# Second layer's experts on sorted token tiles, and attention's mask added by VectorE

## What is computed

```python
a = a * decay + ekv_t          # scan over t, once forwards, once in reverse
b = b * decay + ek_t
num = nf + nb - ekv + euk * vf
den = df + db - ek + euk
out = sigmoid(r) * (num / maximum(den, 1e-8)) * (0.8 + 0.2 * tf)
```

## Time and profile before

| | |
|---|---|
| Median of 3 runs | 1093.78 us (1093.57 to 1094.86) |
| The profiled execution | 1093.23 us, span 1091.4 us |
| TensorE, weight loads | 867.0 us (79%), 668.0 us (61%) |
| VectorE | 675.6 us (62%) |
| ScalarE | 416.4 us (38%) |
| GpSimd | 312.0 us (29%) |
| DMA | 46.51 MB, mean 43 GB/s |

### The profile page before, as it was taken

How to read it: one execution, slowest core, us unless ns; L and a number is a source line. 1 busy time by engine, 2 the same in 40 slices (tenths; PEclk the granted TensorE clock), 3 DMA queues, 4 the chain that set the end, 5 groups by cost and what they waited for, 6 DMA issues and landing times. The chain is left out here.

```text
span 1091.4 us, 12660 instructions
## 1 busy us (share of the span) xinstructions
PE 867.0 (79%) x4116; PEld 668.0 (61%) x4121; DVE 675.6 (62%) x1194; ACT 416.4 (38%) x869; POOL 312.0 (29%) x244
## 2 busy tenths in 40 slices
PE   0677564777888862545999999999997799999996
PEld 0233353655666542235778878887886778888884
DVE  6887896379999988664456555555555333232324
ACT  3201422322323215765445445445444243433432
POOL 0310001135556533421101101100100145555553
PEclk9888796789999995876899999999999599999999
DMA  3000001111211003003011011000000143233331
GB/s 123 1 1 1 0 1 59 69 49 49 84 61 49 20 0 135 0 1 111 6 39 40 1 40 38 15 23 0 0 0 2 58 119 89 57 97 78 82 69 39
DMA packets 31768, 46.51 MB, mean 43 GB/s; under 512 B 18183, under 2 KB 23791, under 8 KB 30056
## 3 DMA queue, kind: packets, MB, share of 16 engines
q1 hardware_dynamic: 31432, 45.76, 13.6%
q10 hardware_dynamic: 288, 0.14, 0.1%
HBM read 44.70 MB, written 1.19 MB: 42 GB/s over the span
## 5 line engine op out<-in xcount | busy, mean ns | idle before, releaser
L2055 DVE TENSOR_TENSOR B_l<-bank,TW_l 128x512 f32<-128x512 f32 (+1 forms) x50 | 34.6, 692 | 140.8 <-PE bank L2000 140.8
L1621 POOL TENSOR_TENSOR WL<-RAW,WH 128x512 fp32r<-128x512 f32 x32 | 41.1, 1289 | 240.7 <-ACT WH L1645 240.7
L1673 ACT ACTIVATE EX<-bank,nm 128x128 f32<-128x128 f32 (+1 forms) x128 | 52.8, 417 | 122.2 <-DVE nm L1719 122.1
L2090 POOL TENSOR_TENSOR HL_l<-H_l,HH_l 128x512 fp32r<-128x512 f32 (+1 forms) x50 | 64.1, 1283 | 118.3 <-ACT HH_l L2069 118.3
L948 POOL TENSOR_TENSOR HL_l<-H_l,HH_l 128x512 fp32r<-128x512 f32 x36 | 52.4, 1456 | 114.9 <-ACT HH_l L914 114.9
L2000 PE MATMUL bank<-XH,WH_l 128*128 128x512 f32 (+1 forms) x200 | 80.0, 400 | 0.0
L2000 PE MATMUL bank<-XL,WH_l 128*128 128x512 f32 (+1 forms) x200 | 79.6, 398 | 0.0
L2000 PE MATMUL bank<-XH,WL_l 128*128 128x512 f32 (+1 forms) x200 | 79.5, 398 | 0.0
L1733 DVE TENSOR_TENSOR AL<-bank,AH 128x256 fp32r<-128x256 f32 x64 | 27.1, 424 | 62.2 <-ACT AH L1688 62.1
L914 ACT ACTIVATE HH_l<-H_l 128x512 fp32r<-128x512 f32 x36 | 22.7, 632 | 107.4 <-DVE H_l L871 107.4
L2077 ACT ACTIVATE S_l<-bank 128x512 f32<-128x512 f32 (+1 forms) x50 | 30.1, 602 | 84.2 <-PE bank L2000 84.2
(11 more groups left out here) (293 smaller groups left out, 2526.6 us busy)
## 6 DMA issues: line engine op xcount, KB each, us to landing
RAW<-l_attn SPq DMA_DIRECT2D x8, 1024.0 KB, 4.9
RAW_l<-l_experts SPq DMA_DIRECT2D x9, 768.0 KB, 4.2
RAW_l<-l_experts SPq DMA_DIRECT2D x9, 512.0 KB, 3.9
TW_l<-routed SPq DMA_DIRECT2D x8, 512.0 KB, 3.6
TW_l<-routed SPq DMA_DIRECT2D x16, 256.0 KB, 5.1
RAW<-l_w SPq DMA_DIRECT2D x3, 1024.0 KB, 7.7
TW_l<-routed SPq DMA_DIRECT2D x14, 192.0 KB, 3.2
RAW_l<-l_experts SPq DMA_DIRECT2D x9, 256.0 KB, 4.4
```

Of the source, the lines that this page charges most:

```text
L1621: pool.tensor_tensor(WL[:, slot, c], RAW[:, slot, c], WH[:, slot, c].bitcast(F32), ALU.subtract).then_inc(w_low, 1)
L1673: act.activation(EX[:, s, a:b], banks[2 + s][:, a:b], ACT.Exp, bias=nm[:, s, i:i + 1], scale=scale, accum_out=rs[:, s, i:i + 1]).then_inc( ...
L2055: v.tensor_tensor(self.B[0:rows, q % 2], self.k.banks[2 * (q % 2) + 1][0:rows], self.TW[0:rows, w % self.TWS, n * W:(n + 1) * W], ALU.mult ...
L2090: pool.tensor_tensor(self.HL[0:rows, q % 4], self.H[0:rows, q % 2], self.HH[0:rows, q % 4].bitcast(F32), ALU.subtract).then_inc(self.h_low, 1)
```

## The change

Gains: the list of double buffers and the helpers that tell a gain's slot and what it waits for are written in another form (gain_summed, gain_sum_no, gain_free); which gain uses which slot, add or identity matmuls stays as it is.

Experts is dropped. layer1 loads the shared expert's weights (WS) and those of all 8 routed experts (WE) at once, with numbers left whole (fp32 matmuls). It zeroes a DRAM buffer of 15 x 128 token rows, counts the tokens of each expert and their ranks by small matmuls, and gives each token a place so that each expert's tokens start at a multiple of 128. GpSimd scatters the transposed, scored tokens there by 8 indirect DMAs. The shared expert's four up steps, each with one gain piece on VectorE behind it, come in between. Then 15 tiles of 128 tokens run through: load, transpose, up with the weights of the tile's expert (whose offset TensorE reads into a register), silu and product, transpose, down, copy, store. The other 28 gain pieces lie behind the products of the tiles. GpSimd then gathers each token's row by 8 indirect DMAs, and TensorE adds shared and routed results.

Attention: the mask is an fp32 tile of 128x256, which VectorE adds to the scores while it takes the maximum, writing the sums to SBUF, from where ScalarE takes the exponentials. TensorE's next scores into a bank wait for that (rowmax) and not for the exponentials. The loop over groups is written out.

```diff
 def gain_slot(c):
-    return c % 2 if c < SUMMED else 0
+    return c % 2 if gain_summed(c) else 0
+def gain_free(c):
+    return max([i + 1 for i in range(c) if gain_slot(i) == gain_slot(c)], default=0)
...
+TILES1 = (T + E1 * (P - 1)) // P
+RING1 = 3
+FIRST_GAIN1 = 2 * NCH
...
+def pieces_after(j):
+    left = len(PIECES1) - STEPS1
+    return PIECES1[STEPS1 + left * j // TILES1:STEPS1 + left * (j + 1) // TILES1]
...
         @block.sync
         def _(sp):
-            ex.load_raw(sp, 0, 0)
             sp.dma_start(RW[:], io["l1_router"]).then_inc(r_in, 16)
...
+            sp.dma_start(WS[:], io["l1_experts"][0]).then_inc(ws_in, 16)
+            sp.dma_start(WE[:].rearrange("p (e c) -> p e c", e=E1),
+                         io["l1_experts"][1:].rearrange("e p c -> p e c")).then_inc(we_in, 16)
+
+            sp.wait_ge(made, 1)
+            sp.dma_start(xs_d.rearrange("(j p) d -> p j d", p=P),
+                         ZERO[:].rearrange("p (o d) -> p o d", o=1).to_broadcast([P, TILES1, D])).then_inc(zeroed, 16)
+
+            def load(j):
+                if j >= RING1:
+
+                    sp.wait_ge(xt_turned, j - RING1 + 1)
+                sp.dma_start(XIN[:, j % RING1], xs_d[j * P:(j + 1) * P]).then_inc(x_in[j % RING1], 16)
+
+            sp.wait_ge(scat, 16 * NT)
+            for j in range(RING1):
+                load(j)
+            for j in range(TILES1):
+                if j + RING1 < TILES1:
+                    load(j + RING1)
+
+                sp.wait_ge(y, j + 1)
+                sp.dma_start(ys_d[j * P:(j + 1) * P], YO[:, j % RING1]).then_inc(y_out[j % RING1], 16)
...
+            pool.wait_ge(zeroed, 16)
+            pool.wait_ge(pos, 10)
+            for t in range(NT):
+
+                pool.wait_ge(xtok, t + 1)
+                pool.indirect_dma_start(xs_d, bass.IndirectOffsetOnAxis(ap=SLOT[:, t:t + 1], axis=0), XTOK[:, t],
+                                        None).then_inc(scat, 16)
+            for c in range(FIRST_GAIN1 + 2, LAYERS * NCH):
+                gain_pool(pool, k, c)
+            for n in range(RING1):
+
+                pool.wait_ge(y_out[n], 16 * len(range(n, TILES1, RING1)))
+            for t in range(NT):
+                pool.indirect_dma_start(YG[:, t], None, ys_d, bass.IndirectOffsetOnAxis(ap=SLOT[:, t:t + 1], axis=0)
+                                        ).then_inc(y_in[t], 16)
...
         @block.scalar
         def _(act):
-            for part in range(3):
-                ex.split_high(act, 0, 1, 0, part)
-            cond_scalar(act, k, cond, XH)
+            cond_scalar(act, k, cond)
...
+            turn(0)
+            for j in range(TILES1):
+                if j + 1 < TILES1:
+                    turn(j + 1)
+
+                act.wait_ge(up, j + 1)
+                if j >= 2:
+                    act.wait_ge(h, j - 1)
+                act.activation(ST[:, j % 2], banks[j % 2][:, 0:F1], ACT.Silu).then_inc(silu, 1)
+                if j >= 1:
+                    product(j - 1)
+                if j >= 2:
+                    result(j - 2)
...
+            for j in range(TILES1):
+
+                v.wait_ge(silu, j + 1)
+                if j >= 2:
+                    v.wait_ge(h_turned, j - 1)
+                v.tensor_tensor(HT[:, j % 2], ST[:, j % 2], banks[j % 2][:, F1:2 * F1], ALU.mult).then_inc(h, 1)
+                for c, what in pieces_after(j):
+                    piece(c, what)
...
+            for j in range(TILES1):
+                if j + 1 < TILES1:
+                    turn(j + 1)
+                at[j] = pe.value_load(EID[0:1, j:j + 1], min_val=0, max_val=(E1 - 1) * WCOLS1)
+                tile_up(j, at[j])
+                if j >= 1:
+                    tile_turn(j - 1)
+                if j >= 2:
+                    tile_down(j - 2, at[j - 2])
+            tile_turn(TILES1 - 1)
+            tile_down(TILES1 - 2, at[TILES1 - 2])
+            tile_down(TILES1 - 1, at[TILES1 - 1])
...
                         for i, (a, b) in enumerate(((0, P), (P, 3 * P))):
-                            v.tensor_reduce(mx[:, s, i:i + 1], banks[2 + s][:, a:b], AX.X, ALU.max).then_inc(rowmax, 1)
+                            v.tensor_tensor_reduce(EX[:, s, a:b], banks[2 + s][:, a:b], MASK[:, 2 * P - (b - a):],
+                                                   1.0, NEG, ALU.add, ALU.max,
+                                                   accum_out=mx[:, s, i:i + 1]).then_inc(rowmax, 1)
...
-                            pe.wait_ge(expd, 2 * (q - 1))
+                            pe.wait_ge(rowmax, 2 * (q - 1))
                         at = b * SEQ
                         out = banks[2 + s]
 
-                        pe.matmul(out[:, 0:P], Q[:, head, at:at + P], K[:, head, at:at + P], start=True, stop=False)
-                        pe.matmul(out[:, 0:P], k.IDB[:], MASK[:], start=False, stop=True)
+                        pe.matmul(out[:, 0:P], Q[:, head, at:at + P], K[:, head, at:at + P], start=True, stop=True)
                         pe.matmul(out[:, P:3 * P], Q[:, head, at + P:at + SEQ], K[:, head, at:at + SEQ],
-                                  start=True, stop=False)
-                        pe.matmul(out[:, 2 * P:3 * P], k.IDB[:], MASK[:], start=False, stop=True).then_inc(scores, 1)
+                                  start=True, stop=True).then_inc(scores, 1)
```

More of the change, by code:

```diff
@@ L1002, in layer1 @@
-        r_in, prio, logits, rt, sc, turned, rows, sent, s_in, xs, xsh, xsl = [
-            sem(n + "_1") for n in ("r_in", "prio", "logits", "route", "score", "turned", "rows", "sent", "s_in",
-                                    "xs", "xsh", "xsl")]
+        HOT = sb("HOT1", [P, NT, E1], BF16)
+        score = sb("score1", [P, NT], F32)
+        need = sb("need1", [P, E1], F32)
+        tiles = sb("tiles1", [P, E1], F32)
+        ends = sb("ends1", [P, E1], F32)
+        begin = sb("begin1", [P, E1], F32)
@@ new lines, in tile_up @@
+            def tile_up(j, at):
+                pe.wait_ge(xt, j + 1)
+                if j >= 2:
+                    pe.wait_ge(h, j - 1)
+                else:
+                    pe.wait_ge(s_h, 4)
+                both = WE[:, bass.ds(at, 2 * UP1)].rearrange("p (o i f) -> p o i f", o=2, i=KD)
+                for i in range(KD):
+                    mm = pe.matmul(banks[j % 2][:], XT[:, j % 2, i * P:(i + 1) * P], both[:, :, i],
+                                   start=(i == 0), stop=(i == KD - 1))
+                mm.then_inc(up, 1)
@@ new lines, in tile_turn, with tile_down @@
+            def tile_turn(j):
+                pe.wait_ge(h, j + 1)
+                if j >= 1:
+                    pe.wait_ge(hf, j)
+                for f in range(2):
+                    mm = pe.transpose(banks[3][:, f * P:(f + 1) * P], HT[:, j % 2, f * P:(f + 1) * P], k.IDF[:])
+                mm.then_inc(h_turned, 1)
+            def tile_down(j, at):
+                pe.wait_ge(hf, j + 1)
+                if j >= 2:
+                    pe.wait_ge(y, j - 1)
+                for f in range(2):
+                    w = WE[:, bass.ds(at + (DOWN1 + f * D), D)]
+                    mm = pe.matmul(banks[4 + j % 2][:, 0:D], HF[:, j % 2, f * P:(f + 1) * P], w,
+                                   start=(f == 0), stop=(f == 1))
+                mm.then_inc(down, 1)
@@ L1130 @@
+            for t in range(NT):
+                pe.wait_ge(y_in[t], 16)
+                for m in range(KD):
+                    mm = pe.matmul(acc[2 * m + t // 4][:, (t % 4) * P:(t % 4 + 1) * P], YG[:, t, m * P:(m + 1) * P],
+                                   k.IDF[:], start=False, stop=(t % 4 == 3), skip_group_check=True)
+            mm.then_inc(acc_sum, 1)
 FF2 = 1024
```

510 lines of the change are left out of this document (206 added, 304 removed).

## The result

The changed kernel takes 1021.6 us (median), against 1094.3 us of the kernel before on the same chip: a ratio of 0.932 (0.930 to 0.935). Three of its four executions took 1019.4 to 1022.1 us and one 2679.1 us in a slower state, which counts in the median of 1021.6 (1021.1 without it) and not in the ratio. The profiled execution took 1019.41 us, span 1017.7. The forecast was 1039 us, in a range of 1008 to 1068.

The account below looks back on a forecast made before the run. It took VectorE to set the pace of the second layer's expert loop and TensorE that of attention. 1093.23 - 47.4 (second layer) - 7.5 (attention) = 1038.3, median 0.55 higher: 1039 us, range 1008 to 1068.

Parts of the forecast that it names:

- rival 1: The forecast itself: second-layer tiles paced by the chain of load, tile, copy, store; 1039 us, own range 1022 to 1056, 55%.
- rival 2: Second-layer tiles: the clock stays up or the load lands soon, cycle 7.0 us; 1013 us, 22%.
- The cycle: Second-layer tiles from tile 4 on: gap 3.5, TensorE 5.6, register read 0.5, together 9.6 us (bounds 7.0 and 11.6).
- signs named for being right: Trace signs: earlier router matmuls, tiles 9 to 10 us apart, 3.5 us idle before turns, clock near 0.7, scans near 0.66.
- The register read: Second-layer tiles: TensorE's read that picks each tile's expert, between 0 and 1.6 us, taken as 0.5 a cycle.
- Up to the first tile: Second layer from its start at 181.95: conditioning, router, ranks, zeroing, scatters and first load; first tile in at 225.
- The indirect DMAs: Second layer: GpSimd's eight scatters and eight gathers, 1.2 us each, the middle between 0.32 and some 2 us.
- Rival 4: Slower than before: GpSimd's 16 indirect DMAs uncovered on the path; gain gone from 4.6 us each, 1116 at 6; 7%.
- Ends: Second layer's close: last tile 5.1 us, store 2.3, eight gathers 9.6, landing 2.6, last sums 0.6.
- VectorE's scans: Second layer: with the splits and so the collisions removed, scans all take near 0.66 us.
- Attention: Mask matmuls removed: 0.13 us x 56 steps of seven dense groups, 7.5 us gained; last group and unrolling 0.
- The sentence on the Trainium skill: Second-layer tiles: a loop waiting for a DMA between bursts runs matmuls cold; wholly cold 6.5 for 5.6, 10 us more.

Follow-up runs that it names:

- Ring5: The changed kernel with five instead of three buffers for the tiles loaded and for those stored: 1008.8 us, ratio 0.922.
- order4: The changed kernel, ring of three kept, with the load of tile j+4 instead of j+3 ahead of the wait for tile j's copy: 1008.5 us.
- hoist_warm: The changed kernel with the register read one iteration earlier and three unread fp32 matmuls ahead of the turns of tiles 4 to 14: 1008.5 us.
- mask_mm: The changed kernel with attention's mask made by identity matmuls as in the kernel before, groups still written out: 1030.4 us.
- warm: The changed kernel with three unread fp32 matmuls of 512 columns ahead of the turns of tiles 4 to 14: 1011.6 us.

## Why the prediction was right, and where its sizes were off

What happened is what it forecast, rival 1: a chain of load, tile, copy and store, with TensorE idle before each turn and VectorE waiting. Ring5 and order4 show it by taking the chain away. But the median is 17 us below the forecast, at the edge of rival 1's own range (1022 to 1056) and between it and rival 2 (1013). The cycle, 7.85 us, lies outside rival 1's own 8.5 to 10.8 and nearer to rival 2's 7.0. Two of the signs named for being right didn't come: a tile every 9 to 10 us, and a clock near 0.7 in the tiles (0.87). The stated range held because it had been drawn to take in rival 2. Nearly all of the miss is in the cycle.

- *The cycle*: 9.6 forecast, 7.85 measured, 17.5 us over ten cycles. Its gap was 3.5 and measured 3.0: the load lands in 2.2 us, near the lower bound of 1.9 and not at the 2.65 taken. TensorE at full clock with the register read was 4.0 and measured 3.9. The clock was given 2.1 us a cycle and costs 0.9: this is the step that failed. The one gap of 4.3 us in the earlier trace rows, behind which TensorE resumed at half clock, was applied to every gap; here TensorE resumes at 2.4 GHz each time, and the clock then falls in six cycles of ten, which take 1.4 to 1.8 us longer than the others. A second term was off as well, the gap, by 0.5 us a cycle.
- *The register read*: 0.5 taken; hoist_warm gives 0.6.
- *Up to the first tile*: 43.05 us from the layer's start forecast, 41.6 measured, out of errors that partly cancel. On the path, the zeroing lands 2 us earlier, the scatters take 11.9 for 9.6, and their landing and the first load are 0.7 shorter each. Off the path, the router's matmuls start 1.35 later than taken (the conditioning's products run beside GpSimd's), and the first shared step takes 3.7 and not 5.4, since the clock is up again. Iterations 0 to 2 and the first gap take 14.6 for 16.0.
- *The indirect DMAs*: 1.2 taken; 1.25 measured for the gathers, 1.5 on average for the scatters, of which some run beside VectorE's work. The 1.2 was the middle between two rows for other transfers, so that it came so close is luck. Rival 4, slower than before, needed 4.6 and is gone.
- *Ends*: the last tile is 2.3 us longer than forecast, as its product waits for VectorE's scans. Below, the turn of the last product (L1062) with 2.0 us of it, the shared down matmuls and the first gather:

```profile
326.16 0.49 PE L1062 MATMUL bank<-IDF,HT 128*128 128x128 f32 x2 [2.02 <-DVE HT L984]
...
330.51 7.13 PE L1101 MATMUL bank<-HS,WS 128*128 128x512 f32 x16 [0.47 <-ACT YO L905]
...
332.98 1.01 POOL L868 DMA_INDIRECT YG<-sorted_y,SLOT  x1 [27.86 <-DMA sorted_y<-YO]
```

- *VectorE's scans* are near 0.66, as said, where the earlier trace rows had 1181 ns for those of NB; only three that meet GpSimd's product are longer, 1.7 us each, which lifts one kind to 878 (groups: busy, mean ns, idle before):

```profile
L178 DVE TENSOR_TENSOR_SCAN DB<-EK,DEC 128x255 f32<-128x255 f32 x14 | 12.3, 878 | 0.0
...
L178 DVE TENSOR_TENSOR_SCAN NB<-EKV,DEC 128x255 f32<-128x255 f32 x14 | 9.2, 658 | 0.0
```

- *Attention*: 0.13 x 56 = 7.5 forecast. The price of a step was right (1.1 a group of eight steps is 0.14), but the last group gains as well: 8.3 over 64. VectorE's longer step is covered, as said.
- *Last experts*: nothing forecast, 1.3 us lost. They are the same code, and all changed kernels take 248.5 to 249.9 us there for 247.3 before. In their first 30 us TensorE's clock is 0.60 before and 0.54 after, but that doesn't settle it: mask_mm has 0.66 there and still takes 248.5, warm 0.60 and takes 249.9. The cause stays open. This and the clock at attention's start nearly cancel.
- *The bookkeeping of the gains*: 0, as said; the third layer, which has only that of the change, takes 92.6 us for 92.9.

The sentence on the Trainium skill (TensorE: Matmul & The Clock Gate, Loop structure matters more than you think), that such a loop runs its matmuls cold, is borne out by half: the tiles run at 0.87, neither cold nor warm, and wholly warm is worth 9 us in ten cycles. The section speaks of a long wait for a DMA between every matmul; here it is 3.0 us ahead of 3.9 us of work. The figure of the other sentence on the Trainium skill (DMA: Bandwidth & Descriptors, Latency and other measured facts), about 1 us, is the time to the first byte of a GpSimd-issued DMA. No run here shows that; the 0.56 us of a plain and the 1.25 of an indirect one are how long each holds GpSimd's queue.

## What to carry to other kernels

In a loop of loads and stores on one queue, ask for every load which wait stands ahead of it, and in which iteration that wait ends: moving the load one place ahead brought as much as two more buffers. A short wait of TensorE in each iteration has two prices, its own length and the clock that falls behind it; the second can eat what a shorter iteration brings, so an edit of under 1 us in such a loop is best timed with the clock held, as in hoist_warm. Once the chain is gone, read which engine is full and give its work to the stretch in which it is idle: that brought another 12 us.

## What the runs showed of the hardware

- Behind equal gaps of 3.0 us TensorE's clock falls to 1.2 GHz in some cycles and not in others, three times about 2 us after it has resumed, three times 0.2 to 0.3 us after. With the register read moved out of the chain, the work from turn to last matmul is shorter (3.3 for 3.9 us), and the mean clock was lower (0.71 for 0.97 from 260 to 280 us); why isn't shown. The same code, run again, had mean cycles of 7.85 and 8.02 us.
- An indirect DMA takes 0.95 us of GpSimd and 0.30 to the next. Beside VectorE's scans and products the same one takes up to 1.55, and one in each of the ten traces with them, which runs beside its additions of 512 columns, takes 2.4 to 3.3. In the changed kernel:

```profile
211.65 0.96 POOL L860 DMA_INDIRECT sorted_x<-XTOK,SLOT  x1 [0.30 <-issue]
212.23 0.69 DVE L198 TENSOR_TENSOR DF<-DF,DB 128x512 f32<-128x512 f32 x1
...
212.92 2.64 POOL L860 DMA_INDIRECT sorted_x<-XTOK,SLOT  x1 [0.30 <-issue]
```

- VectorE's maximum with the mask added comes as two instructions, the second of which reads the accumulator in 83 ns. The first takes 289 ns (128 columns) and 419 (256), no more than the plain maximum of the kernel before with 291 and 415. So on VectorE the mask costs that read:

```profile
L1693 DVE CUSTOM_DVE_ANT_0 EX<-bank,MASK 128x256 f32<-128x256 f32 x64 | 26.8, 419 | 0.0
L1693 DVE CUSTOM_DVE_ANT_0 EX<-bank,MASK 128x128 f32<-128x128 f32 x64 | 18.5, 289 | 24.1 <-PE bank L1784 23.8
L1693 DVE DVE_READ_ACCUMULATOR2_ANT mx<- 128x1 f32 x128 | 10.6, 83 | 0.0
```
